# Rows of x for the first feed-forward stage: indexed transfers from GpSimd's queue in place of the sync engine's loads

## The reference

```python
x = x + 0.5 * ffn(layernorm(x), ...)
x = x + attention(layernorm(x), ...)
x = x + 0.5 * ffn(layernorm(x), ...)

def ffn(x, ...):
    x_mixed = mix(x, mix_kernel)                    # three taps along the sequence
    h = einsum('bsd,pdm->bspm', x_mixed, W1) + b1   # nine paths of 64 columns
    stacked = einsum('bspm,pmd->bspd', h, W2) + b2
    scores = tanh(x_mixed @ Wo1 + bo1) @ Wo2 + bo2
    weights = one_hot(argmax(scores), 9)            # one path a row
    return layernorm_affine(x + einsum('bspd,bsp->bsd', stacked, weights))
```

## Time and profile before

| | us |
|---|---|
| median of 2 runs | 1461.74 |
| lowest and highest run | 1461.27, 1462.22 |
| span of the profiled execution, first to last instruction | 1460.0 |
| PE busy in it | 1336.2 (92%) |
| DVE busy in it | 1178.4 (81%) |
| ACT busy in it | 923.2 (63%) |
| POOL busy in it | 326.0 (22%) |

### The profile page before, as it was taken

How to read it: one execution, slowest core, us unless ns; L and a number is a source line. 1 busy time by engine, 2 the same in 40 slices (tenths; PEclk the granted TensorE clock), 3 DMA queues, 4 the chain that set the end, 5 groups by cost and what they waited for, 6 DMA issues and landing times.

```text
span 1460.0 us, 24657 instructions
## 1 busy us (share of the span) xinstructions
PE 1336.2 (92%) x7700; PEld 773.8 (53%) x7700; DVE 1178.4 (81%) x2326; ACT 923.2 (63%) x1717; POOL 326.0 (22%) x359
## 2 busy tenths in 40 slices
PE   3999998868999999999879999999998879999995
PEld 2567765644454454544344455454544336777764
DVE  5999998876778777788875787787778768989986
ACT  5676764446567666566866567666575866766641
POOL 2255553432010000040011010000130004555422
PEclk9899999979999999999999999999999989999998
DMA  6243333320001100011201010000002211433321
GB/s 157 51 125 109 113 99 91 92 73 0 16 29 36 38 0 29 1 44 38 79 1 44 30 44 16 29 15 15 29 15 74 86 32 51 121 93 108 92 79 58
DMA packets 86985, 82.18 MB, mean 56 GB/s; under 512 B 8539, under 2 KB 86884, under 8 KB 86884
## 3 DMA queue, kind: packets, MB, share of 16 engines
q1 hardware_dynamic: 86884, 80.91, 18.4%
HBM read 55.43 MB, written 25.46 MB: 55 GB/s over the span
## 4 chain that ended last, share of the span: by engine, by line
PE 64%; DVE 15%; issue 9%; ACT 8%; POOL 2%; DMA 1%; DVEq 0%; ACTq 0%; POOLq 0%; SPq 0%
PE PS L1618 57%; DVE R L1047 2%; PE PS L1626 2%; DVE R L1041 2%; PE PS L1716 2%; ACT R L1458 2%; ACT R L1462 2%; DVE run_max L1035 1%; PE PS L1687 1%; DVE x_st L1069 1%; ACT R L1417 1%; POOL R L608 1%; DVE R L852 1%; DVE st L751 1%; DMA R<-in_L_attn_x 1%
## 5 line engine op out<-in xcount | busy, mean ns | idle before, releaser
L1618 PE MATMUL PS<-R 128*128 128x512 f16 (+3 forms) x3456 | 718.4, 362 | 36.1 <-DVE R L1047 29.7
L1618 PEld LDWEIGHTS PS<-R 128*128 128x128 f16 (+1 forms) x3456 | 325.9, 98 | 395.6 <-DVE R L1047 58.8
L1047 DVE TENSOR_TENSOR R<-R 128x512 f16<-128x512 f32 (+3 forms) x288 | 188.7, 655 | 96.1 <-ACT R L1462 94.4
L1449 ACT ACTIVATE R<-PS 128x512 f32 (+5 forms) x288 | 160.3, 558 | 158.8 <-PE PS L1618 158.8
L1458 ACT ACTIVATE R<-R 128x512 f32<-128x512 f32 (+4 forms) x288 | 169.6, 589 | 52.2 <-DVE R L1041 51.3
L1618 PE MATMUL PS<-R,w_hi 128*128 128x512 f16 x640 | 195.5, 388 | 4.3 <-DVE R L801 4.3
L1618 PE MATMUL PS<-w_hi,R 128*128 128x256 f16 x1024 | 189.0, 274 | 10.5 <-DVE R L843 10.5
L1462 ACT ACTIVATE R<-R 128x512 f16<-128x512 f32 (+3 forms) x288 | 171.1, 594 | 26.7 <-ACT R L1458 0.4
L1041 DVE TENSOR_TENSOR R<-R,max_row 128x512 f32<-128x512 f32 (+4 forms) x288 | 186.8, 648 | 0.5 <-ACT max_row L1526 0.5
L1035 DVE TENSOR_TENSOR run_max<-run_max,R 128x512 f32<-128x512 f32 (+3 forms) x272 | 175.6, 645 | 8.4 <-DVE run_max L1035 1.7
L575 POOL TENSOR_SCALAR veps<-mv 128x4 f32<-128x4 f32 x48 | 16.4, 343 | 653.4 <-issue 376.0
(11 more groups left out here) (124 smaller groups left out, 1752.5 us busy)
## 6 DMA issues: line engine op xcount, KB each, us to landing
R<-x_scratch SPq DMA_DIRECT2D x48, 512.0 KB, 4.1
x_scratch<-R SPq DMA_DIRECT2D x32, 512.0 KB, 3.2
R<-oh_scratch SPq DMA_DIRECT2D x32, 320.0 KB
R<-in_L_attn_x SPq DMA_DIRECT2D x16, 512.0 KB, 5.1
R<-oh_scratch SPq DMA_DIRECT2D x32, 256.0 KB
out<-R SPq DMA_DIRECT2D x16, 512.0 KB, 3.2
R<-in_L_ffn_W SPq DMA_DIRECT2D x2, 288.0 KB
R<-in_L_ffn_W SPq DMA_DIRECT2D x1, 512.0 KB
```

Of the source, the lines that this page charges most:

```text
L1047: v.tensor_tensor(p_lo[:, i * TT + lo:(i + 1) * TT], pf[:, (i % 2) * TT + lo:(i % 2 + 1) * TT], p_hi[:, i * TT + lo:(i + 1) * TT], ALU.sub ...
L1449: a.activation(cols(ring, ring_m + i * TT + lo, TT - lo), ps_s[:, i, lo:], ACT.Abs, scale=1.0 / (QS * XS * D ** 0.5)).then_inc(abs_done, 1)
L1618: ins = t_.matmul(dst, w, xx, start=start and n == 0, stop=stop and n == last, skip_group_check=skip)
```

## The change

The loads of x for the first feed-forward stage leave SP's queue. POOL writes a table of row numbers (`row_at`, entry [p, i] = 128 i + p) and fetches each tile by four indexed transfers of 128 rows, one for each of the tile's blocks. Each raises a semaphore of the tile's place (`x_gathered`), and DVE waits for the sum of the four. Tiles 0 to 2 are fetched at the head of POOL's program, tiles 3 to 7 ahead of its first turn, and tiles 8 to 15 behind the turns 1 to 8, after a wait for the step that frees the place. The second feed-forward stage loads as before.

```diff
+            g.iota(row_at[:, :], [[P, NTT * SUB]], base=0, channel_multiplier=1).then_inc(row_at_done, 1)
+
+            def gather_rows(t):
+                for u in range(SUB):
+                    at = t * SUB + u
+                    g.indirect_dma_start(cols(x_rows(t), u * D, D), None, x_flat,
+                                         bass.IndirectOffsetOnAxis(ap=row_at[:, at:at + 1], axis=0))\
+                        .then_inc(x_gathered[t % NT], 16)
+
+            pool.wait_ge(row_at_done, 1)
+            for t in range(3):
+                gather_rows(t)
             g.memset(th[DM:DM + 1, :], 1.0).then_inc(pool_const, 1)
...
+                for t in range(3, NT) if ph == 0 else ():
+                    gather_rows(t)
                 for t in turns():
                     turn(t)
+                    if ph == 0 and on(t - 1) and on(t - 1 + NT):
+                        pool.wait_ge(x1_done, t)
+                        gather_rows(t - 1 + NT)
...
-                for t in range(NT) if ph == 0 else ():
-                    load_rows(t)
-                    if t == 2:
-                        load_weights()
+                if ph == 0:
+                    load_weights()
...
                         if on(t - 1 + NT):
-                            load_rows(t - 1 + NT)
+                            if ph == 1:
+                                load_rows(t - 1 + NT)
...
                     if u == 0:
-                        dve.wait_ge(x_in[t % NT], 16 * loads(ph, t))
+                        if ph == 0:
+                            dve.wait_ge(x_gathered[t % NT], 16 * SUB * (t // NT + 1))
+                        else:
+                            dve.wait_ge(x_in[t % NT], 16 * loads(ph, t))
```

More of the change, by code:

```diff
@@ L59, in macaron @@
     x_t, x1_t, x2_t, out_t = tiles(x), tiles(x1), tiles(x2), tiles(out)
+    x_flat = x.rearrange("b s d -> (b s) d")
     ctx = ExitStack()
@@ L160, in macaron @@
         half = sb("half", [P, SUB])
+        row_at = sb("row_at", [P, NTT * SUB], mybir.dt.uint32)
         th = sb("th", [DM + 1, TT])
@@ L195, in macaron @@
         woT_done, wqk_psum, wvo_psum = sem("woT_done"), sem("wqk_psum"), sem("wvo_psum")
+        row_at_done, x_gathered = sem("row_at_done"), [sem(f"x_gathered{i}") for i in range(NT)]
         x_in = [sem(f"x_in{i}") for i in range(NT)]
@@ L353, in loads @@
         def loads(ph, t):
-            return (ph * (NTT // NT) + t // NT + 1) - (1 if ph == 1 and t % NT < EARLY else 0)
+            return t // NT + 1 - (1 if t % NT < EARLY else 0)
         def early(ph, t):
```

## The result

| | us |
|---|---|
| before, median of 2 runs (lowest, highest) | 1461.74 (1461.27, 1462.22) |
| after, median of 2 runs (lowest, highest) | 1515.99 (1515.99, 1516.00) |
| ratio, with its 95% interval | 1.0372 (1.0342 to 1.0403) |
| span of the profiled execution, before and after | 1460.0 and 1514.2 |

The kernel became 3.7% slower. The forecast was 1507, in a range of 1481 to 1552. I follow the 54.2 us between the two spans. All lines of POOL, DVE and ACT behind the new code have moved by some 20: `veps` is L591 (before L575), the statistics L848 (L824), `result_added` L884 (L860).

What follows compares the result with a forecast made beforehand. The chain bounded the ramp, PE and nearly DVE the steady turns. Span 1460.0 plus 34.4 for the head and 11.2 for the seam gave 1505.6; 1.7 between span and median made 1507 us, range 1481 to 1552.

Steps and rivals of the forecast that it cites:

- The limit: First feed-forward stage: the chain counts in the ramp, PE and DVE are full in steady turns; POOL's 22% average says nothing.
- The price c: Time POOL is taken by one indexed transfer of 128 rows, put at 1.2 us by likeness to POOL's power instruction.
- The first rival: Both places on POOL: it only hands transfers over, at 0.13 to 0.93 us each; no difference to be told; chance 0.20.
- The head: Start of POOL's program: 32 transfers stand ahead of tile 0's scale and delay it, in full on the chain, by 34.4 us.
- The seam: Between turns, tiles 8 to 15: DVE stands 1.65 us for POOL's four transfers, eight times; 11.2 us in all.
- The landing: Between turns: the last transfer's rows land 1.9 us after it is given out.
- The gap: Between turns on POOL: transfers start at about 148.0, after `shift` ends at 147.90.
- the four transfers: Between turns on POOL: all four are given out by 148.0 + 4c, with c = 1.2 us.
- the second rival: Transfers are stretched beside DVE's on-chip work, to 1.8 us each between turns, giving 1526 us; chance 0.22.
- The third rival: Between turns: transfers land as late as the big load did, 4.4 us, giving 1527 us; chance 0.08.
- The hiding of the result's scale and the residual: POOL's work queued behind the transfers between turns ends in time, hidden by 4.35 us of idle time until c = 1.7.
- The rest: Attention and the second feed-forward stage are not touched, only begin later and last as long as before.

Runs made afterwards that it cites:

- experiments 1 and 2: Changed kernel with tiles 8 to 15 loaded by SP as before, 1498.84 us; changed kernel with tiles 0 to 7 loaded by SP as before, 1483.26 us.
- experiment 6: Changed kernel with tiles 0 to 7 fetched by eight indexed transfers of 64 rows each instead of four of 128; 1561.92 us.
- experiment 7: Changed kernel with one plain transfer of 512 rows from POOL for each tile instead of four indexed ones, at the same places; 1466.48 us.
- experiment 5: Changed kernel with only tiles 0 and 1 fetched ahead of POOL's first scale, then one tile behind each of the first six scales; 1491.77 us.
- experiment 3: Changed kernel with DVE's statistics of the new tile moved later in its turn, directly ahead of its moments; 1525.11 us.

## Why the prediction was right, and where it was off

**The limit.** That POOL's average says nothing was right: it rose from 22% to 26% and cost 3.7%. Both losses lie where the text put them, the ramp's chain and DVE's wait at the seam, and experiments 1 and 2 show them apart.

**The price c.** 1.2 was chosen and 1.25 measured. The number was right and the reason given for it was not: by experiment 6 it is no price of 128 addresses, since 64 cost 1.21. That a price by likeness to POOL's power came out within 0.05 was luck, and the total leans on it: by c alone the range ran from 1481 to 1545. The first rival, a mere hand-over, falls (it needed c under 0.94); it describes the plain transfer of experiment 7, with 0.82 for a whole tile and 1466 us. The 1.0 us that were taken there from the Trainium skill ("DMA: Bandwidth & Descriptors", section "Latency and other measured facts") are its figure for the first byte; the trace has 1.25 for what a transfer takes of POOL and 1.80 from its end to DVE's start.

**The head: 34.4 forecast, 36.4 measured, and 0.6 on top.** `veps` at 41.7 became 43.65. Of the 2 us, 32 times 0.05 are 1.6, and 0.36 is the first transfer's start (1.66, where the text has 1.3; its own terms, 0.73, 0.3 and 0.2, add up to 1.23, and the wait for the table alone was 0.63). The ramp behind it was to last as long as before, 45.7; it took 0.6 longer, by the small matmuls, whose two lengths both stand in the trace of before and were not looked for.

**The seam: 11.2 forecast, 18.2 measured.** This is the term that was mis-sized. The wait was to be 1.65 and was 2.59 in the mean. In the turn shown the wait is the gap of 0.48 in front, the transfers of 5.35 with their gaps, and the landing of 1.80, less the 5.12 that DVE leaves: 2.51. The landing (1.9) was right here. The gap (0.1) was not, which is 0.38 a turn, and the four transfers (4.8) were not, which is 0.55. They were 1.09, 1.17, 1.24 and 0.94 long, with 0.30 between them. The 1.09 belongs to the first place behind `shift`, as experiment 5 shows. The 1.17 and 1.24 lie beside DVE's L807 and L815, which have two inputs on chip; the 0.94 lies beside L928, which takes one input from PSUM, and beside DVE's wait. So a stretch of the second rival's kind is there, smaller than it had it: two transfers in four by 0.2 to 0.3, one in 32 to 1.93, not all of them to 1.8. That DVE's instructions do the stretching is read from where they lie and from the 0.95 of the same places without them in experiment 5; the 0.95 at 28.51 and 35.24 there do not fit, and no run took these instructions away. What the prediction held against this rival was misread: in the turn before, DVE is not mostly on PSUM or idle between 147.44 and 153. It runs L786 and L794 there, twice each for 0.74 us, and L901 for 0.68, all with two inputs on chip.

The third rival (landing of 4.4) is out: 1.80 in the turn shown, 1.64 to 1.87 in all eight. In the head, beside the loads of the weights, the fourth transfer ended at 6.63 and DVE started at 9.67, 3.04 later.

**The hiding of the result's scale and the residual** held: `y_rstd` ends at 201.96, and L876, which needs it, starts at 208.22; `residual` ends at 204.32, and the next `veps` on POOL starts at 208.48. It held with help, since DVE's own wait made room. Its condition, c under 1.7, was not the only one: the pair of `residual` and L822 was 0.7 us from meeting, and with the statistics moved in experiment 3 it met. That block was not in the text.

**The rest** was to be as long as before, and it was but for the 0.9 us in one turn whose granted clock was 0.84 before and 0.91 after. With that, 45.6 forecast stand against 54.2 measured: +2.0 head, +0.6 ramp, +7.0 seam, -1.0 tail and rest.

## What to carry to other kernels

An indexed transfer had a price for each instruction on GpSimd here, hardly for each row (1.21 us for 64, 1.25 for 128): count the transfers, multiply, and ask what stands behind them in that engine's program, since the same 32 cost 37 us or 12 by their place alone. At the hand-over inside the loop the landing of the last transfer is what counted (1.8 us after its end as a rule, up to 3.5 beside a load of SP), so the room to look for is between the release of the place and the first read: two transfers fit here, the third added 9.5 us to the eight turns and the fourth 8.7 more. Before an instruction of DVE is moved next to GpSimd's work, look whether both read on chip; a wait that goes can come back as a block of the two.

## What was not expected of the hardware

- The price of an indexed transfer hardly depends on its rows: 0.91 us for 64 rows and 0.95 for 128, with 0.30 us of idle "issue" between two in both; a plain transfer of 512 rows from the same engine takes 0.82 (the median), and no such gap shows between several.
- The first transfer behind `shift` begins 0.48 us after its end and is 1.09 long; the first of the program is 1.21 long.
- Transfers of 1.17 to 1.93 us lie beside DVE's instructions with two inputs on chip, though not every transfer beside one is lengthened. Where `residual` and DVE's L822 meet, it is DVE that takes longer: 2.92 us for 1.21.
- Eight small matmuls of the ramp took 1.06 us before and 1.88 after, both at a granted clock of 1.00; a second such group took 1.88 before at 0.50. What makes it 1.88 at 1.00 was not found.
